# Relation messages in 32 matmuls instead of 48 a tile, with two serial adds on VectorE, and five long loops set at the head of a fetch block

## The chip, the cores and the metric

The kernel runs on one core of one Trainium2 chip. The metric is device microseconds of the whole kernel, one launch. A core has TensorE (PE, with its weight loads shown apart as PEld), VectorE (DVE), ScalarE (ACT), GpSimd (POOL) and the queue engine SP.

## The reference

A graph layer with eight relations, then a mixture of 16 experts with the best two chosen for each node. There are 3125 nodes of 256 features and 53125 edges (50000 drawn ones, both ways of 25000, and one loop for each node), sorted by target.

```
h_all = einsum('ni,roi->rno', layernorm(x), weight)          # 8 relations
messages = segment_sum(h_all[edge_type, src], dst, nodes)
x = x + messages + bias
t = layernorm(x)
probs = softmax(t @ gate_w + gate_b);  best two, weights rescaled to sum 1
h = silu(t @ w1[e]) * (t @ w2[e]);     out = sum over the two of weight * (h @ w3[e])
x = x + out
```

## The kernel before

**Gather stage.** The sum over edges is taken before the product with the relation weights. The nodes are cut into 25 tiles of 125 (`TILES`, `TP`), the sorted edges into 425 chunks of 125, 17 to a turn (`TC`), in six groups of 3, 3, 3, 3, 3 and 2 chunks (`GROUPS`). For each chunk POOL issues one indirect DMA (L486) that gathers 125 rows of the layernormed table `x_tab`, as two float16 halves, into `got`. VectorE builds a one-hot matrix `hot` of target and relation (L877). TensorE multiplies the two into PSUM (`window`, L1253, 12 matmuls for a group of three chunks). VectorE adds the window's sums to the buffer `store` (`add_window`, L895), and right behind that copies the next indices of that group from `gidx` to `idx` (L897), for which POOL waits before it gathers the group of the next turn. So no group is gathered before the add of the group that used its place.

**One turn** i of the loop has the groups (i,3), (i,4), (i,5), (i+1,0), (i+1,1), (i+1,2). When the last add of a tile is done, ScalarE takes the tile's sums out of `store` as the high half (`take_tile`, L634, 128x2048, into `part`), VectorE makes the low half from the rest (`low_tile`, L909, eight instructions), and TensorE multiplies both with the relation weights (`messages`, L1265): 8 relations, 2 halves of the contraction, and three products each, high by weight-high, high by weight-low, low by weight-high, all summed into 256 columns of one PSUM bank. In `add_tile` VectorE then adds that bank to `acc` (L918), takes mean and variance (L921, L924), later normalizes (L928, L932), and TensorE makes the gate logits (L1280, L1286). ScalarE moves the buffer on (L641) and clears its tail (L612).

**Order on the engines.** Everything is written by hand with semaphores, and each engine works in program order. TensorE's turn is: windows (i,3), (i,4), (i,5), transposes, window (i+1,0), gate, messages of tile i-1, windows (i+1,1), (i+1,2). VectorE's turn is: `low_tile` and the adds of (i,3), (i,4), (i,5), (i+1,0), (i+1,1), then `add_tile`, then the add of (i+1,2). ScalarE's take of the next tile waits for that add and for the messages (`tile_summed`). Turns 2 to 23 are a hardware loop of 22 rounds on each of TensorE, VectorE and ScalarE; turn 1 and the last one are written out. POOL's loop has one turn's 17 gathers as its body. The last turn has no groups of a next tile, and takes the messages of two tiles one behind the other.

**Expert stage.** Rows are sorted by expert into `xs_tab`, and for 58 slots of 128 rows TensorE makes the up products (L1387), transposes (L1395, L1355) and the down products (L1369). It is a loop over pairs of slots on TensorE, VectorE and ScalarE.

The lines that decide the order within `turn` on VectorE:

```python
if at == len(groups) - 1 and parts and not last:
    add_tile(n, node_tile(i - 1, b, single))
if at == 0 and parts:
    low_tile(n)
    buffer_moved(v0 + i)
add_window(v0, t, g, w, v0 + i, second if at < HALF else first)
```

Of the kernel before, what the change touches and what calls it, by code (L numbers as in the profile page):

```python
# [30 lines left out]
ALU = mybir.AluOpType  # L31
# [4 lines left out]
NODES, DIM, RELS = 3125, 256, 8  # L36
# [3 lines left out]
KT = DIM // P  # L40
HT = HIDDEN // P
TP = 125
TILES = NODES // TP
# [47 lines left out]
def build(nc, x, src, dst, etype, w_rel, b_rel, gate_w, gate_b, w1, w2, w3, out):  # L91
# [5 lines left out]
    with ExitStack() as ctx:  # L97
# [3 lines left out]
        def sem(name):  # L101
            return ctx.enter_context(nc.semaphore(name))
# [13 lines left out]
        acc = sb("acc", [TP, TILES, DIM])  # L116
# [22 lines left out]
        wT = part_flat[:, 0:4 * RO].rearrange("p (h k n) -> p h k n", h=2, k=KT)  # L139
# [101 lines left out]
        ps = ctx.enter_context(nc.psum_tensor("ps", [P, 8, QW], F32))  # L241
# [48 lines left out]
        tile_high = sem("tile_high")  # L290
        tile_low = sem("tile_low")
        tile_summed = sem("tile_summed")
        acc_added = sem("acc_added")
        stats2_raw = sem("stats2_raw")
        stats2_begun = sem("stats2_begun")
# [169 lines left out]
        def _(pool):  # L465
# [26 lines left out]
            gather_turn(0)  # L492
            pool.wait_ge(counts_ready, 5)
            visits = pool.value_load(n_visits[0:1, 0:1], min_val=TILES, max_val=TILES * TILES * GEN_W)
            with pool.Fori(1, visits) as n:
                gather_turn(n)


# [51 lines left out]
            pairs = pool.value_load(pairs_i[0:1, 0:1], min_val=EXPERTS // 2, max_val=SLOT_TILES // 2)  # L550
# [22 lines left out]
        def _(act):  # L573
# [27 lines left out]
            for n in range(8):  # L601
                k, rp = n // 4, n % 4
# [53 lines left out]
            with act.Fori(0, tiles_n) as b:  # L656
                with act.Fori(0, wins_n) as w:
                    v0 = (b * GEN_W + w) * TILES
                    move_on(v0, (v0 + 1) * NG + HALF)
                    clear_old(v0)  # L660
                    spread(v0)
                    move_on(v0 + 1, (v0 + 2) * NG + HALF)
                    keep_x2(v0, 0, b)
                    clear_old(v0 + 1)
                    with act.Fori(2, TILES - 1) as i:
                        spread(v0 + i - 1)
                        move_on(v0 + i, (v0 + i + 1) * NG + HALF)
                        keep_x2(v0 + i - 1, i - 1, b)
                        clear_old(v0 + i)
                    t = TILES - 1  # L670

                    take_tile(v0 + t, (v0 + t + 1) * NG, last_high)
                    spread(v0 + t - 1)
                    keep_x2(v0 + t - 1, t - 1, b)
                    spread(v0 + t)
                    keep_x2(v0 + t, t, b)
                    shift(v0 + t)
                    clear_old(v0 + t)
# [42 lines left out]
            pairs = act.value_load(pairs_i[0:1, 0:1], min_val=EXPERTS // 2, max_val=SLOT_TILES // 2)  # L721
            high_xs(0, 0)
            expert_tile(0, 0, first=True)
            expert_tile(0, 1)
            with act.Fori(1, pairs) as i:
                for u in range(2):
                    expert_tile(i, u)
            act.wait_ge(y_done, final_j + 1)
# [8 lines left out]
        def _(dve):  # L737
# [13 lines left out]
            v = nc.vector  # L751
# [161 lines left out]
            def tile_at(table, tile):  # L913
                return table[0:TP, bass.ds(tile, 1), :].rearrange("p a d -> p (a d)")

            def add_tile(n, tile, bank=MSG_BANK):
                dve.wait_ge(tile_summed, n + 2)
                v.tensor_tensor(tile_at(acc, tile), tile_at(acc, tile), ps[0:TP, bank, 0:DIM], ALU.add).then_inc(acc_added, 1)  # L918
                dve.wait_ge(acc_added, n + 2)
                dve.sem_inc(stats2_begun, 1)  # L920
                v.bn_stats(stat2[0:TP, :], tile_at(acc, tile)).then_inc(stats2_raw, 1)  # L921
                dve.wait_ge(stats2_raw, n + 1)
                dve.sem_inc(stats2_begun, 1)
                v.bn_aggr(mv2[0:TP, :], stat2[0:TP, :]).then_inc(stats2_done, 1)  # L924
# [94 lines left out]
            with dve.Fori(0, tiles_n) as b:  # L1019
                with dve.Fori(0, wins_n) as w:  # L1020
# [12 lines left out]
                    dve.wait_ge(bias_added, (b * GEN_W + w + 1) * X_LOADS)  # L1033
                    dve.sem_inc(stats2_begun, 1)
                    turn(v0, 1, b, w, norm=False)
                    with dve.Fori(2, TILES - 1) as i:
                        turn(v0, i, b, w)
                    turn(v0, TILES - 1, b, w, last=True)
                    n = v0 + TILES - 1
# [145 lines left out]
                step(v.tensor_tensor(mtx[:, :], wts[:, 1, :], is_low[:, 1 - k, :], ALU.mult))  # L1185
                step(v.tensor_tensor(wts2[:, k, :], wts2[:, k, :], mtx[:, :], ALU.add))
            v.tensor_copy(pos2[0:TP, :, :], low_hi[:, :, :]).then_inc(pos2_done, 1)
            with dve.Fori(1, pairs) as i:
                for u in range(2):
                    expert_tile(i, u)  # L1190
            low_hid(final_j)
# [15 lines left out]
        def _(pe):  # L1207
# [49 lines left out]
            def messages(n, bank=MSG_BANK, high=tileT[:, 0, :, :, :], low=tileT[:, 1, :, :, :]):  # L1257

                pe.wait_ge(tile_low, n + 2)
                if bank == MSG_BANK:  # L1260
                    pe.wait_ge(acc_added, n + 1)
                for r in range(RELS):
                    for k in range(KT):
                        for a, b in PARTS:
                            last = mm(ps[:, bank, 0:DIM], (high, low)[a][:, k, r, :], wT[:, b, k, r * DIM:(r + 1) * DIM],  # L1265
                                      start=(r == 0 and k == 0 and a + b == 0), stop=(r == RELS - 1 and k == KT - 1 and a == 1))
                last.then_inc(tile_summed, 1)

            def ranks(t0, t1):
# [149 lines left out]
            turn_xs(0, 0, first=True)  # L1419
            expert_tile(0, 0, first=True)  # L1420
            expert_tile(0, 1)
            with pe.Fori(1, pairs) as i:
                for u in range(2):
                    expert_tile(i, u)
            turn_hid(final_j)
# [21 lines left out]
```

## Time and profile before

| what | value |
|---|---|
| time, median of 3 runs | 1306.32 us (1306.45, 1306.32, 1300.31) |
| time of the profiled execution | 1302.33 us |
| its span, first to last instruction | 1300.6 us |
| mean granted TensorE clock | 0.789 of full |
| busy PE / DVE / ACT / POOL | 65% / 47% / 27% / 52% |

The span is one execution, the table's time is that execution's own. Clock is in parts of 2.4 GHz. Busy shares are means over stages with different limits; no engine is busy all the time, so it is the waits that have to be read.

### The profile page before, as it was taken

Reading aid. Unit: us, or ns where it says so; the run is one execution under the profiler, and the core shown is the slowest. Engines: PE = TensorE matmul, PEld = TensorE weight load, DVE = VectorE, ACT = ScalarE, POOL = GpSimd, SP = SyncE. Lnnn points to the kernel's source line nnn. Section 1 sums busy time; section 2 is a strip of 40 time slices with the busy share of each in tenths; the row PEclk is TensorE's granted clock in tenths of the full one; section 3 lists DMA queues with packets and bytes.
Section 4 is the critical chain, followed back from the end, with each engine's and each line's share of the span. In section 5 each row is a group of like instructions: output and inputs, shape, how many; then the busy total and the mean of one; then the engine's idle time right before and its main releaser. Section 6 shows DMA issues by size and latency. Waiting matters only on the chain.

```text
span 1300.6 us, 19171 instructions
## 1 busy us (share of the span) xinstructions
PE 845.9 (65%) x4904; PEld 689.7 (53%) x4905; DVE 607.5 (47%) x1597; ACT 345.9 (27%) x397; POOL 670.0 (52%) x621
## 2 busy tenths in 40 slices
PE   1256677766677766677666677437897988897600
PEld 1134455555555545555555556326786877786500
DVE  6655454445555444444545555674333333333432
ACT  4502223333222222222333323312222222222100
POOL 1366455554555555545555452056444477738373
PEclk9967777777777777777877777658998988999855
DMA  9523333333333222232222321316625364454244
GB/s 223 168 88 107 102 97 102 103 105 108 118 96 96 77 77 76 76 90 69 77 77 77 88 69 33 117 51 224 202 73 185 97 196 158 150 194 109 82 132 124
DMA packets 93629, 145.98 MB, mean 112 GB/s; under 512 B 13367, under 2 KB 67595, under 8 KB 93610
## 3 DMA queue, kind: packets, MB, share of 16 engines
q0 software_dynamic: 25968, 70.94, 18.9%
q1 hardware_dynamic: 50794, 59.48, 14.3%
q10 hardware_dynamic: 16848, 15.34, 3.6%
q8 instruction: 7, 0.11, 0.0%
q14 instruction: 12, 0.10, 0.0%
HBM read 109.90 MB, written 33.98 MB: 111 GB/s over the span
## 4 chain that ended last, share of the span: by engine, by line
PE 22%; issue 19%; DVE 18%; another core or an unknown queue 16%; ACT 8%; DVEq 7%; DMA 5%; POOL 4%; ACTq 1%; SPq 0%; POOLq 0%
PE ps L1387 6%; PE ps L1265 5%; ACT part L634 5%; PE ps L1369 4%; DVE part L909 4%; PE ps L1253 4%; DVE hot L877 3%; DMA y_tab<-ffn 3%; DVE store L895 3%; DVEq L895 2%; POOL x_sb L556 2%; POOL store L567 1%; PE ps L1395 1%; ACT hot L592 1%
## 5 line engine op out<-in xcount | busy, mean ns | idle before, releaser
L486 POOL DMA_INDIRECT got<-x_tab,idx x425 | 405.2, 953 | 379.2 <-DVE idx L897 237.8
L1253 PE MATMUL ps<-hot,got 125*128 125x256 f16 x1700 | 296.5, 328 | 135.8 <-issue 125.1
L1253 PEld LDWEIGHTS ps<-hot,got 125*128 125x128 f16 x1700 | 187.6, 115 | 236.5 <-issue 187.6
L895 DVE TENSOR_TENSOR store<-store,ps 128x512 f32 x150 | 102.8, 685 | 293.2 <-remote 151.0
L1265 PE MATMUL ps<-part 128*128 128x256 f32 x1152 | 191.2, 341 | 24.8 <-DVE part L909 24.8
L1265 PEld LDWEIGHTS ps<-part 128*128 128x128 f32 x1152 | 186.4, 251 | 27.4 <-DVE part L909 27.3
L1387 PE MATMUL ps<-part,operands 128*128 x696 | 183.6, 415 | 1.2 <-DVE operands L1142 1.2
L1387 PEld LDWEIGHTS ps<-part,operands 128*128 128x128 f32 x696 | 134.0, 199 | 28.3 <-issue 1.8
L909 DVE SCALAR_TENSOR_TENSOR part<-store,part 128x256 fp32r<-128x256 f32 x192 | 103.0, 613 | 66.6 <-ACT part L634 42.1
L619 ACT ACTIVATE dev<-mv,eps 125x1 f32<-125x1 f32 x25 | 7.4, 294 | 474.0 <-DVE mv L924 474.0
L1369 PE MATMUL ps<-part,operands 128*128 x696 | 103.4, 301 | 39.1 <-DVE operands L1152 34.5
L877 DVE TENSOR_SCALAR hot<-key_row,pass,drel 125x256 f16<-125x256 f16 x425 | 122.1, 351 | 6.0 <-issue 6.0
L1369 PEld LDWEIGHTS ps<-part,operands 128*128 128x128 f32 x696 | 92.0, 202 | 42.9 <-issue 42.8
L634 ACT ACTIVATE part<-store 128x2048 fp32r x24 | 94.2, 3926 | 63.4 <-DVE store L895 63.4
L509 POOL TENSOR_TENSOR part<-store,part 128x2048 fp32r<-128x2048 f32 (+1 forms) x28 | 97.8, 3493 | 2.3
L507 POOL TENSOR_SCALAR part<-store 128x2048 fp32r<-128x2048 f32 (+1 forms) x28 | 41.5, 1482 | 103.1 <-PE ps L1387 87.1
L699 ACT CAST operands<-ps 128x512 fp32r<-128x512 f32 x58 | 34.1, 587 | 193.7 <-DVE ffn L1148 123.8
L1152 DVE TENSOR_TENSOR operands<-ps,operands 128x512 fp32r<-128x512 f32 x58 | 40.1, 691 | 81.8 <-ACT operands L699 76.9
L1286 PE MATMUL ps<-gw_sb,x2T 128*125 128x16 f32 x100 | 21.9, 336 | 79.5 <-ACT x2T L628 79.5
L520 POOL DMA_INDIRECT x_sb<-x_tab,oct_idx x64 | 61.1, 954 | 23.4 <-issue 17.1
L1148 DVE COPY ffn<-ps 128x256 f32<-128x256 f32 x58 | 24.6, 424 | 90.3 <-PE ps L1369 42.5
L1286 PEld LDWEIGHTS ps<-gw_sb,x2T 128*125 128x125 f32 x100 | 19.3, 273 | 86.8 <-ACT x2T L628 86.8
(198 smaller groups left out, 743.7 us busy)
## 6 DMA issues: line engine op xcount, KB each, us to landing
store<-in_L_ffn_w SPq DMA_DIRECT2D x48, 512.0 KB
xs_tab<-x_sb SPq DMA_DIRECT2D x16, 512.0 KB
y_tab<-ffn SPq DMA_DIRECT2D x9, 896.0 KB
ffn<-xs_tab ACTq DMA_DIRECT2D x59, 128.0 KB
y_tab<-ffn ACTq DMA_DIRECT2D x58, 128.0 KB
got<-x_tab,idx POOLq DMA_INDIRECT x425
acc<-in_x SPq DMA_DIRECT2D x5, 560.0 KB
x_tab<-got SPq DMA_DIRECT2D x5, 560.0 KB
```

The costliest lines, as they stand in the source:

```text
L486: nc.gpsimd.indirect_dma_start(got[:, c, :], None, x_tab, bass.IndirectOffsetOnAxis(ap=idx[:, c:c + 1], axis=0)).then_inc(gathered[c], 16)
L507: nc.gpsimd.tensor_scalar(high, whole, 1.0, 0.0, ALU.mult, ALU.add).then_inc(split_high, 1)
L509: nc.gpsimd.tensor_tensor(part[:, 2 * k + 1, at:at + cols], whole, high.bitcast(F32), ALU.subtract).then_inc(done, 1)
L520: nc.gpsimd.indirect_dma_start(xg[:, u, :], None, x2_tab, bass.IndirectOffsetOnAxis(ap=oct_idx[:, u:u + 1], axis=0)).then_inc(oct_got[u // ...
L634: nc.scalar.activation(high, buffer(v, 0, P * RELS).rearrange("p k (n r) -> p k r n", r=RELS), ACT.Copy, scale=1.0 / SCALE).then_inc(tile_ ...
L877: v.tensor_scalar(hot[0:CE, g % HOT, c - GROUPS[g][0], :], key_row[0:CE, :], pass0[0:CE, 0:1], drel[0:CE, bass.ds(turn * TC + c, 1)], ALU. ...
L895: v.tensor_tensor(window, window, ps[:, WIN_BANK[g], :].rearrange("p (k n) -> p k n", k=KT), ALU.add).then_inc(win_added, 1)
L909: last = v.scalar_tensor_tensor(out=low[:, k, rels, :], in0=whole_sums[:, rels, :], scalar=1.0 / SCALE, in1=high[:, k, rels, :].bitcast(F3 ...
L1253: last = mm(ps[:, WIN_BANK[g], k * KEYS:(k + 1) * KEYS], got[0:CE, c, a * DIM + k * P:a * DIM + (k + 1) * P], hot[0:CE, g % HOT, c - c0, : ...
L1265: last = mm(ps[:, bank, 0:DIM], (high, low)[a][:, k, r, :], wT[:, b, k, r * DIM:(r + 1) * DIM], start=(r == 0 and k == 0 and a + b == 0), ...
L1369: last = mm(ps[:, Y_BANK, 0:DIM], hidT[:, a, k, :], part3[:, bass.ds(at + b, 1), k, :].rearrange("p a n -> p (a n)"), start=(k == 0 and a ...
L1387: last = mm(ps[:, UP_BANK + w, :], xsT[:, a, k, :], part12[:, bass.ds(at + b, 1), w, k, :].rearrange("p a n -> p (a n)"), start=(k == 0 an ...
```

## The change

The change has three parts.

- `messages`: the high half now multiplies weight-high and weight-low in one matmul of 512 columns into the whole bank (`both`), and the low half adds its product to the bank's second 256 columns. That is 16 matmuls of 512 columns and 16 of 256, for 48 of 256, with 32 weight loads for 48. The columns that pass are 12,288 in both. It is done for all 25 tiles.
- `add_tile`: since the sum now lies in two halves of the bank, VectorE adds them to `acc` one after the other, the second add behind a wait for the first (`high_added`) and one more increment of `stats2_begun`. 25 times.
- Loops: the gather loops of POOL, ScalarE and VectorE, and the expert loops of ScalarE, VectorE and TensorE are made with `head_slot` 0, which sets the first instruction of the body at the head of a block of instructions. TensorE's gather loop had it already.

```diff
@@ gather loop, POOL @@
-            with pool.Fori(1, visits) as n:
+            with nc.Fori(1, visits, engines=bass.OrderedEngineSet([pool.engine]), head_slot={pool.engine: 0}) as n:
                 gather_turn(n)
@@ gather loop, VectorE (ScalarE alike, and the three expert loops alike) @@
-                    with dve.Fori(2, TILES - 1) as i:
+                    with nc.Fori(2, TILES - 1, engines=bass.OrderedEngineSet([dve.engine]), head_slot={dve.engine: 0}) as i:
                         turn(v0, i, b, w)
@@ add_tile @@
                 dve.wait_ge(tile_summed, n + 2)
-                v.tensor_tensor(tile_at(acc, tile), tile_at(acc, tile), ps[0:TP, bank, 0:DIM], ALU.add).then_inc(acc_added, 1)
+                v.tensor_tensor(tile_at(acc, tile), tile_at(acc, tile), ps[0:TP, bank, 0:DIM], ALU.add).then_inc(high_added, 1)
+                dve.wait_ge(high_added, n + 1)
+                dve.sem_inc(stats2_begun, 1)
+                v.tensor_tensor(tile_at(acc, tile), tile_at(acc, tile), ps[0:TP, bank, DIM:], ALU.add).then_inc(acc_added, 1)
                 dve.wait_ge(acc_added, n + 2)
@@ messages @@
+                both = ps[:, bank, :].rearrange("p (h d) -> p h d", h=2)
                 for r in range(RELS):
                     for k in range(KT):
-                        for a, b in PARTS:
-                            last = mm(ps[:, bank, 0:DIM], (high, low)[a][:, k, r, :], wT[:, b, k, r * DIM:(r + 1) * DIM],
-                                      start=(r == 0 and k == 0 and a + b == 0), stop=(r == RELS - 1 and k == KT - 1 and a == 1))
+                        mm(both, high[:, k, r, :], wT[:, :, k, r * DIM:(r + 1) * DIM],
+                           start=(r == 0 and k == 0), stop=False)
+                        last = mm(ps[:, bank, DIM:], low[:, k, r, :], wT[:, 0, k, r * DIM:(r + 1) * DIM],
+                                  start=False, stop=(r == RELS - 1 and k == KT - 1))
                 last.then_inc(tile_summed, 1)
```

On TensorE, in the body of the gather loop, the place between window (i+1,0) and window (i+1,1) read before (`part` is the tile's high or low half, `ps` PSUM, and REGISTER_ALU and ISA are the sequencer's own steps):

```order
L1247 ISA
L1249 ISA
L1253 MATMUL ps<-hot,got 128x256 x12
L1265 MATMUL ps<-part 128x256 x48
L1246 REGISTER_ALU
L1247 REGISTER_ALU
L1253 MATMUL ps<-hot,got 128x256 x12
```

and begins now, the pair of the fourth and fifth row coming 16 times:

```order
L1251 ISA
L1253 ISA
L1257 MATMUL ps<-hot,got 128x256 x12
L1269 MATMUL ps<-part 128x512
L1271 MATMUL ps<-part 128x256
L1269 MATMUL ps<-part 128x512
L1271 MATMUL ps<-part 128x256
```

Nothing but the messages themselves moved; the windows stand where they stood.

On VectorE the end of a turn, from the one-hots ahead of `add_tile` to the add of window (i+1,2), read before:

```order
L877 TENSOR_SCALAR hot<-key_row,pass,drel 125x256 x2
L918 ISA
L918 TENSOR_TENSOR acc<-acc,ps 125x256
L921 BN_STATS stat<-acc 125x6
L924 BN_AGGR mv<-stat 125x2
L892 REGISTER_ALU
L893 REGISTER_ALU
L895 REGISTER_ALU x2
L895 ISA
L895 TENSOR_TENSOR store<-store,ps 128x2x256
```

and reads now:

```order
L878 TENSOR_SCALAR hot<-key_row,pass,drel 125x256 x2
L919 ISA
L919 TENSOR_TENSOR acc<-acc,ps 125x256
L922 TENSOR_TENSOR acc<-acc,ps 125x256
L925 BN_STATS stat<-acc 125x6
L928 BN_AGGR mv<-stat 125x2
L893 REGISTER_ALU
L894 REGISTER_ALU
L896 REGISTER_ALU x2
L896 ISA
L896 TENSOR_TENSOR store<-store,ps 128x2x256
```

One row of work came in, between the first add and the statistics, and everything behind it moved down by one.

## Rows read from the trace of the kernel before

**Rows 1.** One turn by windows: us, busy time of PE, PEld, DVE, ACT, POOL, clock, DMA

```profile
470.80:500.90 30.10, 20.09 (x124) 15.61 (x122) 14.49 (x43) 8.66 (x7) 16.11 (x18) 0.77 0.25 74
```

**Rows 2.** Waits over the whole span: total us, times, longest

```profile
DVE store L895 <- remote: 151.0, 13, 12.2
```

**Rows 3.** Timeline of VectorE, one turn: start, us, work, idle before and releaser

```profile
494.31 0.69 DVE L895 TENSOR_TENSOR store<-store,ps 128x512 f32 x1 [11.95 <-remote]
...
495.51 0.41 DVE L918 TENSOR_TENSOR acc<-acc,ps 125x256 f32 x1
496.09 0.43 DVE L921 BATCH_NORM_STATS2 stat<-acc 125x6 f32 x1 [0.16 <-DVE acc L918]
...
497.23 0.69 DVE L895 TENSOR_TENSOR store<-store,ps 128x512 f32 x1 [0.38 <-issue]
497.84 0.21 DVE L897 COPY idx<-gidx 125x3 int32 x1
497.94 0.16 DVE L928 RECIPROCAL rstd<-dev 125x1 f32<-125x1 f32 x1
...
502.30 4.29 DVE L909 SCALAR_TENSOR_TENSOR part<-store,part 128x256 fp32r<-128x256 f32 x8 [2.72 <-issue]
506.50 0.69 DVE L895 TENSOR_TENSOR store<-store,ps 128x512 f32 x1
```

**Rows 4.** Timeline of ScalarE, the same turn

```profile
498.17 3.93 ACT L634 ACTIVATE part<-store 128x2048 fp32r x1 [0.99 <-DVE store L895]
```

**Rows 5.** Timeline of POOL, the first and eleventh gather, and the next first

```profile
477.91 0.95 POOL L486 DMA_INDIRECT got<-x_tab,idx  x1 [4.99 <-DVE idx L897]
...
490.49 0.95 POOL L486 DMA_INDIRECT got<-x_tab,idx  x1 [0.30 <-issue]
...
508.06 0.95 POOL L486 DMA_INDIRECT got<-x_tab,idx  x1 [4.99 <-DVE idx L897]
```

**Rows 6.** Timeline of TensorE, the same turn, messages and one window matmul

```profile
476.50 7.51 PE L1265 MATMUL ps<-part 128*128 128x256 f32 x48 [0.75 <-DVE part L909]
...
488.65 0.28 PE L1253 MATMUL ps<-hot,got 125*128 125x256 f16 x1 [0.43 <-issue]
```

**Rows 7.** Timeline of the last loop turn, gathers and VectorE's wait

```profile
779.30 0.95 POOL L486 DMA_INDIRECT got<-x_tab,idx  x1 [4.99 <-DVE idx L897]
...
788.11 0.95 POOL L486 DMA_INDIRECT got<-x_tab,idx  x1 [0.30 <-issue]
...
791.46 0.69 DVE L895 TENSOR_TENSOR store<-store,ps 128x512 f32 x1 [7.71 <-remote]
```

**Rows 8.** Timeline of another loop turn, TensorE and VectorE

```profile
243.62 3.96 PE L1253 MATMUL ps<-hot,got 125*128 125x256 f16 x33
...
253.27 0.69 DVE L895 TENSOR_TENSOR store<-store,ps 128x512 f32 x1 [12.17 <-remote]
```

**Rows 9.** Timeline of TensorE in the expert stage

```profile
953.30 3.02 PE L1387 MATMUL ps<-part,operands 128*128 x12
956.15 0.38 PE L1355 MATMUL ps<-ident,ffn 128*128 128x128 f32 x2
956.29 1.62 PE L1369 MATMUL ps<-part,operands 128*128 x12
957.74 0.60 PE L1395 MATMUL ps<-ident,ffn 128*128 128x128 f32 x4
```

**Rows 10.** Clock of that stretch, by windows, columns as in the first group

```profile
950.00:975.00 25.00, 25.00 (x156) 22.07 (x155) 10.32 (x19) 7.22 (x15) 15.91 (x11) 1.00 0.24 77
```

**Rows 11.** Page, part 3: instruction queues, packets, MB, share

```profile
q8 instruction: 7, 0.11, 0.0%
q14 instruction: 12, 0.10, 0.0%
```

**Rows 12.** Timeline of the gather stage's end

```profile
815.44 8.53 PE L1265 MATMUL ps<-part,operands 128*128 128x256 f32 x48 [3.63 <-DVE operands L909]
...
825.72 0.42 DVE L918 TENSOR_TENSOR acc<-acc,ps 125x256 f32 x1
```

More of the change, by code:

```diff
@@ L292, in build @@
         tile_summed = sem("tile_summed")
+        high_added = sem("high_added")
         acc_added = sem("acc_added")
@@ L664, in _ @@
                     clear_old(v0 + 1)
-                    with act.Fori(2, TILES - 1) as i:
+                    with nc.Fori(2, TILES - 1, engines=bass.OrderedEngineSet([act.engine]), head_slot={act.engine: 0}) as i:
                         spread(v0 + i - 1)
@@ L724, in _ @@
             expert_tile(0, 1)
-            with act.Fori(1, pairs) as i:
+            with nc.Fori(1, pairs, engines=bass.OrderedEngineSet([act.engine]), head_slot={act.engine: 0}) as i:
                 for u in range(2):
@@ L1187, in _ @@
             v.tensor_copy(pos2[0:TP, :, :], low_hi[:, :, :]).then_inc(pos2_done, 1)
-            with dve.Fori(1, pairs) as i:
+            with nc.Fori(1, pairs, engines=bass.OrderedEngineSet([dve.engine]), head_slot={dve.engine: 0}) as i:
                 for u in range(2):
@@ L1421, in _ @@
             expert_tile(0, 1)
-            with pe.Fori(1, pairs) as i:
+            with nc.Fori(1, pairs, engines=PE_ONLY, head_slot={pe.engine: 0}) as i:
                 for u in range(2):
```

## The prediction

> **What bounds the kernel now.** I read the kernel by stages first and then one loop turn engine by engine. A turn of the gather loop takes 30.10 us, and in it no engine is busy throughout: TensorE 20.1 us, POOL 16.1, VectorE 14.5, ScalarE 8.7 [rows 1]. So the turn is a ring of waits, and the question is which. The list of waits puts one on top that no engine of the page explains: VectorE's window add stands still before a releaser called remote, up to 12.2 us at a time [rows 2], and the timeline shows the same wait once a turn, 11.95 us in the one that I take as specimen [rows 3]. There are 22 such loop turns, the starts of which lie 30.10 to 30.19 us apart.
>
> The ring can be walked. VectorE wakes at 494.31, adds window (i+1,1), adds the messages at 495.51, takes the statistics at 496.09 and 496.67, and adds window (i+1,2) at 497.23 [rows 3]. That add releases ScalarE, which takes the tile from 498.17 for 3.93 us [rows 4]. VectorE's eight instructions of the low half start at 502.30, right behind it, and take 4.29 us, the next window add follows at 506.50 and its index copy at 507.09 [rows 3]. That copy releases POOL, which starts its burst of gathers at 508.06 after 4.99 us of idleness [rows 5]. In the turn before the same burst began at 477.91, and its eleventh gather started at 490.49, so they follow at 12.58/10 = 1.26 us; then POOL stops, and VectorE wakes 3.82 us after that last start [rows 3, 5].
>
> What VectorE waits for is TensorE: the messages and window (i+1,1). But the messages' records end at 476.50 + 7.51 = 484.01 [rows 6], more than 10 us before VectorE wakes. Two other turns show that the wake hangs on the burst of gathers, not on the matmuls. In the last loop turn only 8 gathers are issued, 779.30 to 788.11, and the wait is 7.71 us in place of 11.95 [rows 7], so 4.24 us less for three gathers less, which are 3 x 1.26 = 3.8 us. The wake there is 791.46 - 788.11 = 3.35 us after the last gather's start, near the 3.82. And in another turn TensorE ran through 33 window matmuls by 243.62 + 3.96 = 247.58, and VectorE still woke only at 253.27, after 12.17 us [rows 8]. So TensorE's completion reaches VectorE only when POOL's burst is over. I don't know the mechanism; the rows show the order. The period then is: burst of 11 gathers and its tail, 494.31 - 477.91 = 16.4 us, plus VectorE, ScalarE, VectorE from wake to the next burst, 508.06 - 494.31 = 13.75 us. They add up to 30.15.
>
> **The change part by part.**
>
> *The second add.* It lies between 495.51 and 496.09, inside the 13.75 us. Each instruction behind it waits for its result, and the window add that releases ScalarE stands behind all of them on VectorE. Its price is one step of this chain. The nearest row is the add itself with the wait behind it: 496.09 - 495.51 = 0.58 us, of which 0.41 is the add [rows 3]. The statistics behind it, also a dependent step, take the same 0.58 (496.09 to 496.67). The lower bound is 0.41, if the wait for the first add costs nothing; the upper one 0.58 + 0.16 = 0.74, if the additional increment costs another of the gaps seen there. I take 0.58. Can it hide? The idle time of 0.38 us ahead of 497.23 is sequencer work (four register steps stand there in the listing) that begins only when the last wait has passed, so it moves along. ScalarE has nothing else that ends later, VectorE's own idle time of 2.72 us ahead of 502.30 is a wait for ScalarE and starts and ends later too. POOL's second burst, from 495.86, hangs on a copy ahead of the add and isn't touched; it has 4.99 us of slack before the next burst, which becomes 5.57. So the whole 0.58 goes into each period. 22 loop turns and the written-out turn 1 give 23 x 0.58 = 13.3 us. At the end of the stage two more tiles are added; for the last one the add at 825.72 stands behind its messages [rows 12] and ahead of the last layernorm, so one more 0.58, while the other add lies beside the messages from 815.44 on and costs nothing. Sum: **+13.9 us**, bounds 24 x 0.41 = 9.8 and 24 x 0.74 = 17.8.
>
> The Trainium skill ("VectorE: DVE Perf Modes", the section on the TRN2 errata) speaks against this part: each VectorE instruction pays a fixed extra latency, so one tile cut in two pays it twice. By its cycle table an add of 256 columns from PSUM is (120 + 256)/0.96 = 392 ns, by my estimate from that page 24 x 0.39 = 9.4 us in sum; the row has 410 ns for the instruction and 0.58 us for the step with its wait, and the sum above goes by the row.
>
> *The joined messages.* In the expert stage at granted clock 1.00 (2.4 GHz) [rows 10], twelve 512-column matmuls pass in 956.15 - 953.30 = 2.85 us, 0.2375 each, and twelve of 256 columns in 957.74 - 956.29 = 1.45 us, 0.121 each [rows 9]. So a tile's messages go from 48 x 0.121 = 5.81 us to 16 x 0.2375 + 16 x 0.121 = 5.74 us: 0.07 us. In the loop turns they run at mixed clock, 7.51 us, and end 10 us before the wait that follows them ends. The gain is hidden there. At the end of the stage the messages of the last tile are on the path, 8.53 us for 48 at the lower clock [rows 12], 0.178 each; columns are the same, so the bounds are 0 and, if every removed instruction were worth a fixed part of it, 16 x (0.178 - 256/1200 x 0.5) = 1.1 us per tile. I take 0.2 for both last tiles: **-0.2 us**.
>
> *The loop heads.* If a loop lay badly across blocks of instructions, this would show at its back edge or on the instruction queues. VectorE passes its back edge between 497.84 and 497.94, two instructions 0.10 us apart, closer than the 0.21 us of the first [rows 3]. POOL's gathers stand at one pitch throughout. The queues of instructions moved 7 and 12 packets in the whole span [rows 11], far fewer than the 22 rounds. So there is nothing to gain in a round. Each loop is entered once, past some padding; if an entry costs a fetch, that is six times at most 1 us from a full wait of the kind of 0.3 to 1 us seen at entries. The lower bound is a gain of nothing, the upper 6 us; most entries lie beside other engines' waits. I take **+1**.
>
> Sum: 13.9 - 0.2 + 1 = 14.7 us. On the profiled execution's own 1302.33 us (span 1300.6) that gives 1317.0; that execution lies 4.0 us under the median of the runs, from which one gets 1321.0. Two of the three runs lie at 1306.4 and one at 1300.3, so I set the forecast between the two, at **1319 us**.
>
> **The rivals.**
>
> *The shorter messages let TensorE's signals through (faster).* 32 fewer instructions (16 matmuls, 16 weight loads) stand per tile between window (i+1,0) and window (i+1,1). If what holds the completion back is a full queue ahead of TensorE that drains slowly under the burst, fewer entries could let window (i+1,1) complete before the burst is over. For it: under the burst TensorE's window matmuls do appear singly, and the wait starts right with the burst. The Trainium skill ("TensorE: Matmul & The Clock Gate", the text on engine queue depths) gives TensorE a queue of 64 entries; a tile's messages were 96 entries and are now 64. Against it: in the turn of rows 8 the matmuls were through at 247.58 and the wake still came at the burst's end. Its price: VectorE would wake up to when the windows are ready, bounded by POOL, whose 17 gathers at 1.26 us take 21.4 us; a turn could fall from 30.1 to some 22 to 24, 6 us x 22 = -132 us, so about 1185 with the added step. If only the two or three last entries matter, 2 us a turn, 1319 - 44 = 1275. It decides from 0.58 us a turn on. Chance 0.14.
>
> *The second add finds cover (no change).* If the wake in fact follows something that doesn't hang on VectorE's chain, say ScalarE's or the clock of the DMA queues, the 0.58 goes into VectorE's 11.95 us of idleness. Then +0 to +3 from the entries: 1303 to 1309. For it: that idleness is large. Against: the burst begins with the index copy (4.99 us of idleness before it, released by it), and the wait shrank when the burst was shorter. Chance 0.12.
>
> *The loop heads do more than nothing.* If the loops' position matters each round, by fetch stalls hidden in the gaps called issue, 0.3 us a round for 22 + 28 rounds is 15 us, in either sign, since a head moved is also a tail moved. The Trainium skill ("Runtime: NRT & Kernel Launch", the section on instruction fetch) has a taken branch out of the two blocks at hand stall for a fetch. The 19 instruction packets of the span are too few for that in 50 rounds. As a gain it would cancel the add: 1304, chance 0.04; as a loss, 1334, chance 0.04.
>
> **How the numbers follow.** The forecast case has the rest, 0.66, and its own range from 1302.33 + 9.8 - 2.2 = 1310 to 1306.32 + 17.8 + 5 = 1329. The range for 8 in 10 leaves out the case of the passed signals (0.14) and the loss by loop heads (0.04), and reaches down to the no-change case: 1303 to 1329. Half a percent, 6.5 us, is about what a measurement of this kernel can tell from no change: slower than 1312.9 counts as slower. Slower: 0.66 less a sliver of 0.03 that stays under the bound, and the 0.04, 0.67. Same: 0.12 + 0.04 + 0.03, less a part that falls faster, 0.18. Faster: 0.15.
>
> **What would show it.** The two adds should stand 0.58 us apart once a turn, and the idle time of VectorE before a remote releaser should stay at 11.9 us, the eleven gathers at 1.26 us, the turn at 30.7 us. The messages' record of a turn should be as long as now within 0.3 us. A remote wait shorter than 11 us with the burst unchanged would prove the first rival; turns of 30.1 us the second; instruction packets in the hundreds or gaps at the loops' ends the third. I would be wrong most widely if fewer entries in TensorE's queue unblock the windows.

## The result, and the profile after

The changed kernel takes 1314.83 us (median of 5 runs, 1310.95 to 1316.49), the kernel before 1305.49 us in its 5 runs beside it. The ratio is 1.0074 with a 95% interval of 1.0053 to 1.0095: slower, by 9.3 us. The profiled execution took 1315.28 us with a span of 1313.6 us, 13.0 us over the span before. The forecast was 1319 us, in a range of 1303 to 1329.

The experiments need one thing more: the machine was found in two conditions. The kernel before took 1300 to 1306 us in the runs of this section, and 1296 to 1311 us beside e7 to e10; beside e1 to e6 it took 1056 to 1067 us. The runs of one kernel that were timed together lie within 1.4% of each other. Every comparison below is within one condition, and they are called **the 1300 condition** and **the 1060 condition**.

One turn of the loop after, by windows (us, busy PE, PEld, DVE, ACT, POOL, clock, DMA share, GB/s):

```profile
478.00:508.55 30.55, 20.64 (x105) 15.00 (x103) 14.95 (x44) 8.72 (x7) 16.19 (x18) 0.75 0.25 73
```

VectorE in that part of the timeline, which answers to [rows 3]:

```profile
501.64 0.69 DVE L896 TENSOR_TENSOR store<-store,ps 128x512 f32 x1 [11.80 <-PE ps L1257]
...
502.85 0.41 DVE L919 TENSOR_TENSOR acc<-acc,ps 125x256 f32 x1
503.41 0.42 DVE L922 TENSOR_TENSOR acc<-acc,ps 125x256 f32 x1
503.98 0.43 DVE L925 BATCH_NORM_STATS2 stat<-acc 125x6 f32 x1
...
505.12 0.69 DVE L896 TENSOR_TENSOR store<-store,ps 128x512 f32 x1 [0.38 <-issue]
...
510.17 4.28 DVE L910 SCALAR_TENSOR_TENSOR part<-store,part 128x256 fp32r<-128x256 f32 x8 [2.65 <-issue]
```

And POOL, which answers to [rows 5], with the first gather of the last loop turn [rows 7]:

```profile
485.39 0.95 POOL L487 DMA_INDIRECT got<-x_tab,idx  x1 [5.51 <-DVE idx L898]
...
497.98 0.94 POOL L487 DMA_INDIRECT got<-x_tab,idx  x1 [0.30 <-issue]
...
515.91 0.95 POOL L487 DMA_INDIRECT got<-x_tab,idx  x1 [5.50 <-DVE idx L898]
...
791.00 0.95 POOL L487 DMA_INDIRECT got<-x_tab,idx  x1 [5.51 <-DVE idx L898]
```

The profile names TensorE's window as the releaser here, and "remote" in the turn of [rows 3]; in the kernel before it puts the same wait of 11.9 us down to either in about half of the turns, so the name says nothing.

The two adds start 0.56 us apart, the statistics 0.57 us behind the second. From wake to next burst it is 515.91 - 501.64 = 14.27 us where it was 13.75; the medians over the loop's turns are 14.28 and 13.75. But from the burst's first gather to the wake it is 501.64 - 485.39 = 16.25 us where it was 16.40: the burst is as long as before (12.59 us from first to eleventh), and the time from the eleventh gather to the wake is 3.66 us for 3.82. In the medians it is 16.27 for 16.39 us, and 3.70 for 3.82. Over ten turns the period is (791.00 - 485.39)/10 = 30.56 us, before (779.30 - 477.91)/10 = 30.14: 0.42 us a turn, 9.2 us in 22.

The rest of the 13.0 us lies around the loop. The first gather starts 0.48 us later (48.77 for 48.29). From it to the last loop turn it takes 11.2 us more, 2.0 more than the 9.2; 0.9 us of that lie in the first three turns, and most of the rest in two neighbouring turns of the after-trace, which together took 1.3 us more than two others. The end of the stage, from 791.00 to the last add at 837.34, is not longer (46.3 us for 46.4). The expert stage up to the last down products is 1.2 us longer (1237.41 for 1224.62).

The messages, which answer to [rows 6], are now pairs; the first and the last of a turn's 32:

```profile
483.99 0.79 PE L1269 MATMUL ps<-part 128*128 128x512 f32 x1 [1.16 <-DVE part L910]
...
492.07 0.28 PE L1271 MATMUL ps<-part 128*128 128x256 f32 x1
```

8.36 us, for 7.51, both at mixed clock. That is the scatter of single turns: over 20 turns of each trace the median is 8.08 us for 8.05, with 7.1 to 8.7 us in single ones. There is no gain, and the records end more than 9 us ahead of the wake in either.

### The profile page after: what moved, and what is told of

Its sections match the earlier page's. It is cut to its first block, busy times and chain, and to the rows that moved or that the text cites. A ratio compares the mean times of both kernels' runs of the same rounds, so it can differ in the third digit from the quotient of the medians.

```text
span 1313.6 us, 18427 instructions
## 1 busy us (share of the span) xinstructions
PE 841.9 (64%) x4504; PEld 660.7 (50%) x4505; DVE 619.2 (47%) x1622; ACT 344.9 (26%) x397; POOL 670.6 (51%) x621
## 4 chain that ended last, share of the span: by engine, by line
PE 25%; DVE 19%; issue 18%; another core or an unknown queue 16%; DVEq 7%; DMA 6%; POOL 3%; ACT 3%; ACTq 1%; SPq 0%; POOLq 0%
PE ps L1393 7%; PE ps L1257 5%; PE ps L1375 5%; DMA y_tab<-ffn 4%; PE ps L1269 4%; DVE part L910 4%; DVE hot L878 4%; DVEq L896 2%; PE ps L1271 2%; POOL x_sb L557 2%; DVE store L896 2%; POOL store L568 2%; PE ps L1401 1%; ACT part L635 1%
## 5 line engine op out<-in xcount | busy, mean ns | idle before, releaser
L1257 PE MATMUL ps<-hot,got 125*128 125x256 f16 x1700 | 288.4, 328 | 135.3 <-issue 106.2
L1269 PE MATMUL ps<-part 128*128 128x512 f32 x384 | 186.5, 509 | 25.1 <-DVE part L910 25.1
L1271 PE MATMUL ps<-part 128*128 128x256 f32 x384 | 129.1, 336 | 0.0
L1269 PEld LDWEIGHTS ps<-part 128*128 128x128 f32 x384 | 97.2, 253 | 52.3 <-DVE part L910 27.6
L1271 PEld LDWEIGHTS ps<-part 128*128 128x128 f32 x384 | 97.4, 254 | 0.0
```

Source lines behind the costliest of these rows:

```text
L1257: last = mm(ps[:, WIN_BANK[g], k * KEYS:(k + 1) * KEYS], got[0:CE, c, a * DIM + k * P:a * DIM + (k + 1) * P], hot[0:CE, g % HOT, c - c0, : ...
L1269: mm(both, high[:, k, r, :], wT[:, :, k, r * DIM:(r + 1) * DIM], start=(r == 0 and k == 0), stop=False)
L1271: last = mm(ps[:, bank, DIM:], low[:, k, r, :], wT[:, 0, k, r * DIM:(r + 1) * DIM], start=False, stop=(r == RELS - 1 and k == KT - 1))
```

## The experiments

### The 1060 condition: each part alone

`e1_heads` is the kernel before with the loop heads. They are six, and not five as the title has it: those of the gather loops of POOL, ScalarE and VectorE, and those of the expert loops of ScalarE, VectorE and TensorE. `e2_no_heads` is the changed kernel without them.

> The kernel before with the six loop heads alone. My theory (the heads do nothing in a round): turn of the gather loop stays at 30.14 us, the time within 2 us of the kernel before (ratio 0.999 to 1.002). Rival (the heads cost or give something each round): with the chain of the second add taken off, a turn would move by 0.1 us or more, 2.5 us or more in the gather stage, or the expert stage would by 1 us.

> The changed kernel without the loop heads: joined messages and the two adds. My theory: all of the loss is here, turn 30.55 us, +9 to +12 us over the kernel before, ratio 1.007 to 1.009. Rival (heads carry part of it): +6 us or less.

`e3_extra_add` leaves the 48 messages as they were and gives `add_tile` a second, dependent add of zeros:

```diff
-                v.tensor_tensor(tile_at(acc, tile), tile_at(acc, tile), ps[0:TP, bank, 0:DIM], ALU.add).then_inc(acc_added, 1)
+                v.tensor_tensor(tile_at(acc, tile), tile_at(acc, tile), ps[0:TP, bank, 0:DIM], ALU.add).then_inc(high_added, 1)
+                dve.wait_ge(high_added, n + 1)
+                dve.sem_inc(stats2_begun, 1)
+                v.tensor_tensor(tile_at(acc, tile), tile_at(acc, tile), zero[0:TP, 0:1].to_broadcast([TP, DIM]), ALU.add).then_inc(acc_added, 1)
```

> The kernel before, its 48 messages unjoined, with a second dependent add on VectorE (of zeros) behind the first. My theory (the step on the ring costs 0.57 us a turn, and the shorter messages take 0.12 to 0.15 back): wake to next burst 14.3 us, tail of the burst 3.82 us, turn 30.70 us, +12.5 to +14 us. Rival (the tail shrank by chance or for another reason than the messages): turn 30.55 us, like the changed kernel.

`e4_one_add` is the changed kernel, heads included, with the second add left out.

> The changed kernel with only the first of the two adds; it leaves out the sum of the bank's second half (high by weight-low and low by weight-high). My theory: wake to next burst back at 13.75 us, tail 3.70 us, turn 30.0 us, so 2 to 4 us faster than the kernel before (ratio 0.997 to 0.999). Rival (the loss comes from the 512-column matmuls or the heads, not from the add): turn above 30.3 us.

Both kernels were also run unchanged, again in the 1060 condition:

> The kernel before, unchanged, for its trace beside the other runs of this chip. The four runs so far were all some 240 us faster than the trace before: POOL issues its 425 gathers there without a pause and no remote wait stands in a turn. Theory: the state goes with the chip, and this trace shows the same as they do, turns of about 22.1 us, a span of 1056 to 1066 us. If it shows turns of 30.1 us, the state is not the chip's.

> The changed kernel, unchanged. If POOL issues without a pause as in the four runs, the turn is bounded by the larger of POOL's 17 gathers (22.07 us in the run with one add) and the ring with the second add (22.65 us in the runs with two): 22.6 us a turn, and a ratio of 1.011 to 1.013 like the run without heads; if the heads cost the 6 us that their run alone seemed to show, 1.016 to 1.018. With turns of 30.5 us: 1.007.

| kernel | heads | adds | messages | ratio to before (95%) | turn, us |
|---|---|---|---|---|---|
| b_again | no | 1 | 48 | (one run, 1055.56 us) | 22.00 |
| e1_heads | yes | 1 | 48 | 1.0063 (1.0037 to 1.0088) | 22.09 |
| e4_one_add | yes | 1 | 32 | 1.0055 (1.0028 to 1.0083) | 22.07 |
| e2_no_heads | no | 2 | 32 | 1.0115 (1.0084 to 1.0145) | 22.61 |
| e3_extra_add | no | 2 | 48 | 1.0116 (1.0084 to 1.0148) | 22.65 |
| a_again | yes | 2 | 32 | 1.0197 (1.0160 to 1.0233) | 22.54 |

A turn is here the start of gather 409 less that of gather 35, over 22. Each ratio is against the kernel before that was timed beside it; for a_again that was another set of runs than for e1 to e4. A second add costs 0.5 to 0.65 us a turn and 1.15%, with joined messages or without. The joined messages alone give nothing (e2 against e3, e4 against e1). The heads cost 0.6%, some 6 us, and a turn with them is as long as one without, within 0.1 us. Together that is 1.8%, and a_again's 2.0% agrees within its interval.

The turns of 30 us that I had expected did not occur here. Of the times, e1 (expected within 2 us) and e4 (expected 2 to 4 us faster) both came out 6 us slower, e2 came out 12.7 us slower where I expected 9 to 12, and e3, at 12.7 us, lay in its 12.5 to 14. What e3 was to tell of the tail of the burst it could not, since this condition has no such tail.

What bounds a turn here? One turn of the kernel before by windows, and VectorE's window add that had the remote wait:

```profile
311.40:333.40 22.00, 15.67 (x123) 13.28 (x122) 14.96 (x44) 9.86 (x7) 16.82 (x18) 0.90 0.45 130
```

```profile
438.93 0.69 DVE L895 TENSOR_TENSOR store<-store,ps 128x512 f32 x1 [3.10 <-PE ps L1253]
```

The wait is 3.10 us for 11.95, POOL pauses nowhere in the loop for more than 0.3 us, where it paused 4.99 in [rows 5], and no wait called remote is in the list of waits. With the second add POOL does stand still once in the turn shown. POOL and VectorE of `e3_extra_add`:

```profile
443.30 0.94 POOL L487 DMA_INDIRECT got<-x_tab,idx  x1 [1.22 <-DVE idx L898]
```

```profile
430.23 0.41 DVE L919 TENSOR_TENSOR acc<-acc,ps 125x256 f32 x1
430.79 0.43 DVE L922 TENSOR_TENSOR acc<-acc,zero 125x256 f32 x1 [0.15 <-DVE acc L919]
431.36 0.43 DVE L925 BATCH_NORM_STATS2 stat<-acc 125x6 f32 x1
```

So with one add the turn sits at POOL's issue (17 gathers at 1.25 us, two or three of them longer, 22.0 us), and with two the ring of VectorE and ScalarE is just longer (22.6 us). That is a reading of the traces; the run that was to test it, e9, fell in the other condition. The step is 0.56 us in this condition too.

### Where the heads cost

The 6 us do not lie in the gather loop. From the last add to the last down products e1, e4, e6 and a_again take 372 to 376 us, and b_again, e2, e3 and e5, which have no heads, take 362 to 370. Slot by slot it is one step: from VectorE's copy of the first slot's result to its copy of the second's it takes 11.6 to 12.8 us with heads and 6.4 to 7.2 us without; the median slot takes 4.8 to 4.9 us in all of them. ScalarE and VectorE there, of `a_again`:

```profile
711.40 0.59 ACT L700 CAST operands<-ps 128x512 fp32r<-128x512 f32 x1 [8.02 <-issue]
```

```profile
712.31 0.69 DVE L1156 TENSOR_TENSOR operands<-ps,operands 128x512 fp32r<-128x512 f32 x1 [4.79 <-ACT operands L700]
```

and ScalarE of `e2_no_heads`:

```profile
705.47 0.59 ACT L700 CAST operands<-ps 128x512 fp32r<-128x512 f32 x1 [3.05 <-DVE ffn L1152]
...
711.89 0.59 ACT L700 CAST operands<-ps 128x512 fp32r<-128x512 f32 x1 [3.69 <-DVE ffn L1152]
```

In the one ScalarE stands still for 8 us as its loop begins; in the other it has done a slot meanwhile. The records of the loops' own lines show what happens. The branches of `a_again` in the two loops, from the view of one source line (count, shortest, median and longest ns, first and last start in us):

```profile
L726 ACTq COMPARE_BRANCH  x29: 40/45/55, 705.3 to 1011.4; - x29
```

```profile
L1192 DVEq COMPARE_BRANCH  x29: 47/56/69, 707.4 to 1010.5; - x29
```

and those of `e2_no_heads` in ScalarE's:

```profile
L726 ACTq COMPARE_BRANCH  x28: 40/45/50, 716.5 to 1003.2; - x28
```

With a head there is one branch more, and it is at the entry. Behind it ScalarE's sequencer records nothing for 5.92 us (705.33 to 711.25) and VectorE's nothing for 4.73 us (707.47 to 712.20), and the next record of either is a register operation that waits for no semaphore. In the five traces with ScalarE's head this gap is 5.5 to 5.9 us, in the six with VectorE's (e7 is one) 4.5 to 5.7 us. Behind the entries of the other four loops with a head it is at most 0.7 us. So two entries stall, one beside the other, and VectorE's ends 0.9 to 1.9 us after ScalarE's.

The changed kernel shows the same in the 1300 condition, and the kernel before shows something else at that place. ScalarE after:

```profile
903.87 0.59 ACT L700 CAST operands<-ps 128x512 fp32r<-128x512 f32 x1 [9.01 <-issue]
```

ScalarE before:

```profile
888.51 0.59 ACT L699 CAST operands<-ps 128x512 fp32r<-128x512 f32 x1 [3.31 <-remote]
895.62 0.60 ACT L708 ACTIVATE ffn<-ps 128x512 f32<-128x512 f32 x1 [6.53 <-remote]
```

To see whether ScalarE's head is the cause I took that one alone back:

> The changed kernel with all loop heads but the one of ScalarE's expert loop. All four traces with heads have ScalarE standing still for 8 to 9 us ahead of L700 in the second slot, called issue, and the step from the first to the second slot takes 12 us or more where it takes 6.4 to 7.2 us without heads. Theory: ScalarE's entry into its expert loop, past the padding, costs it some 6 us once. Then this kernel shows a step of 6.4 to 7.2 us, and 5 to 7 us less than the changed kernel on the same chip (ratio to before 1.012 to 1.014 with POOL without a pause). Rival (another engine's head, or each round pays a little): step stays at 12 us, ratio 1.018 to 1.021.

This run fell in the 1300 condition. Ratio 1.0068 (1.0043 to 1.0093) against 1.0074 of the full change: nothing gained. ScalarE of `e7_no_act_head`:

```profile
898.40 0.59 ACT L700 CAST operands<-ps 128x512 fp32r<-128x512 f32 x1 [4.47 <-remote]
...
905.54 0.60 ACT L709 ACTIVATE ffn<-ps 128x512 f32<-128x512 f32 x1 [6.55 <-remote]
```

and VectorE:

```profile
903.95 0.69 DVE L1156 TENSOR_TENSOR operands<-ps,operands 128x512 fp32r<-128x512 f32 x1 [5.03 <-issue]
```

The 9.01 us of issue are gone from ScalarE, so its head does make its stall. But VectorE kept its head and its stall. And ScalarE has the kernel before's wait of 6.5 us again, which falls on eight gathers that POOL issues at that time, and which ends 1.6 us after VectorE's stall. In the 1300 condition the stalls of both heads lie beside that wait and cost nothing that shows. So e7 could not tell the price of ScalarE's head. What is shown is that the six heads together cost 6 us in the 1060 condition (e1). That it is these two entries follows from the place and the size, and as the two stalls overlap, taking one back would not give 6 us either; no run in the 1060 condition took one back alone.

The Trainium skill ("Runtime: NRT & Kernel Launch", the section on instruction fetch) says that a taken branch to a target outside the two blocks at hand has to wait for a fetch. The traces agree with it. In all five traces with ScalarE's head a packet of 8 KB on the instruction queue q14 starts 1.5 to 1.8 us ahead of ScalarE's first record behind the gap, and in the six with VectorE's one starts 1.9 to 2.0 us ahead of VectorE's; e7 has only the second, and `e2_no_heads` has no such packet from 701 to 710 us. The page of the changed kernel counts four more on that queue, and one fewer on q8, than [rows 11]:

```profile
q14 instruction: 16, 0.13, 0.0%
```

### The second add off the ring

`e8_adds_behind` is the changed kernel without heads, in another order. `e9_before_adds_behind` is the kernel before in that order.

```diff
 VectorE, turn:
-                    if at == len(groups) - 1 and parts and not last:
-                        add_tile(n, node_tile(i - 1, b, single))
                     ...
                     add_window(v0, t, g, w, v0 + i, second if at < HALF else first)
+                    if at == len(groups) - 1 and parts and not last:
+                        add_tile(n, node_tile(i - 1, b, single))
 ScalarE, loop:
-                        spread(v0 + i - 1)
-                        move_on(v0 + i, (v0 + i + 1) * NG + HALF)
+                        move_on(v0 + i, (v0 + i + 1) * NG + HALF, v0 + i - 1)   # take, then spread, then shift
```

VectorE also builds its one-hots ahead of `normalize2` now.

> Joined messages and two adds, no heads, but the adds and statistics behind the add of window (i+1,2), ScalarE's square root behind its take, VectorE's one-hots ahead of the normalization. This takes four steps of 0.57 us off the ring and puts some 1.1 us of normalization into it. Theory (the second add costs because it stands on the ring): in turns of 22.6 us the ring falls under POOL's 22.07 us and the turn goes to 22.07 to 22.15, ratio to before 1.000 to 1.003, where the same kernel with the adds ahead had 1.0115. In turns of 30 us: 1.2 us less a turn than with the adds ahead. Rival (the cost is the add's work, not its place): 22.65 us, ratio 1.011.

> The kernel before with the same order: one add, behind the window add. Theory: where POOL issues without a pause the turn stays at POOL's 22.05 us, so no change within 0.3%. In turns of 30.1 us: 0.6 us less a turn, 14 us (ratio 0.988 to 0.992). Rival (POOL is not the bound in these turns but the ring is at 22.05 by chance): 21.4 to 21.5 us a turn, 12 us less.

Both ran beside e7 in the 1300 condition, and both are faster than the kernel before: 0.9834 (0.9799 to 0.9870) and 0.9866 (0.9835 to 0.9896). A turn is 1.3 us shorter where I expected 1.2, and 0.8 where I expected 0.6. VectorE of `e8_adds_behind`:

```profile
486.44 0.69 DVE L896 TENSOR_TENSOR store<-store,ps 128x512 f32 x1 [11.86 <-remote]
...
487.83 0.69 DVE L896 TENSOR_TENSOR store<-store,ps 128x512 f32 x1
...
488.50 0.42 DVE L919 TENSOR_TENSOR acc<-acc,ps 125x256 f32 x1
489.07 0.42 DVE L922 TENSOR_TENSOR acc<-acc,ps 125x256 f32 x1 [0.15 <-DVE acc L919]
...
493.66 4.30 DVE L910 SCALAR_TENSOR_TENSOR part<-store,part 128x256 fp32r<-128x256 f32 x8
```

and ScalarE:

```profile
488.76 3.90 ACT L635 ACTIVATE part<-store 128x2048 fp32r x1 [20.73 <-DVE store L896]
```

The window add stands 1.39 us behind the wake, where it stood 3.48 (505.12 - 501.64); ScalarE's take runs while VectorE adds. Of the 2.1 us that this takes off, 0.8 come back, which I put down to the normalization that now stands in the ring. From wake to the next burst it is 499.42 - 486.44 = 12.98 us, 1.3 less than after. The turn is 29.25 us (median of the loop's turns) against 30.55 in e7. With the order changed, the kernel with two adds and 32 messages (29.25 us) is no slower than the one with one add and 48 (29.38). From wake to the next burst both take the same, 12.99 us and 13.00 us in the medians, where after and before had 14.28 and 13.75. So the second add costs only where it stands on the ring. The 0.13 us between the turns are the tail of the burst: 3.69 to 3.71 us from the last gather to the wake in the three kernels with 32 messages in this condition, 3.81 and 3.82 in the two with 48. These three also have the second add, so that it is the messages that shorten the tail is likely, but no run separates the two.

### The burst

If VectorE's wake hangs on the end of POOL's burst, fewer gathers in the burst must bring it earlier. In `e5_late_copy` (kernel before), `e6_late_copy_changed` and `e10_behind_late_copy` (on e8) group 0's indices are copied together with group 1's:

```diff
-                v.tensor_copy(idx[0:CE, c0:c1], gidx[...c0, c1 - c0)]).then_inc(idx_ready, 1)
+                if g > 0:
+                    first_c = 0 if g == 1 else c0
+                    v.tensor_copy(idx[0:CE, first_c:c1], gidx[...first_c, c1 - first_c)]).then_inc(idx_ready, 2 if g == 1 else 1)
```

> The kernel before with the index copy of group (i+1,0) joined to that of (i+1,1), so that POOL's burst before VectorE's wake has 8 gathers for 11, and 9 behind it. In turns of 30.1 us: my theory (the wake hangs on the end of the burst) gives 3.8 us less a turn, 26.3 us, some 80 us less in all (ratio 0.93 to 0.95); the rival (TensorE's matmuls bound the wake) gives no change. In turns of 22 us, where POOL is without a pause: the copy comes before POOL has done the 8, so no change within 3 us, or up to 1 us a turn slower if it comes late.

> The changed kernel with the same joined copy. In turns of 30.5 us: 26.7 us a turn, the difference to the other kernel with the joined copy still 0.4 us a turn. In turns of 22.6 us: as the changed kernel within 3 us, or up to 1 us a turn slower.

These two fell in the 1060 condition, which has no burst with a pause behind it, and say nothing on it: 1.0028 (1.0013 to 1.0044) and 1.0270 (1.0251 to 1.0290, where a_again had 1.0197). The joined copy cost 4 us on the kernel before and 8 us on the changed one.

> The kernel with the adds behind the window add, and the index copy of group (i+1,0) joined to that of (i+1,1): POOL issues 8 gathers ahead of VectorE's wake and 9 behind it. In turns with the remote wait (29.25 us before this edit): theory (the wake hangs on the end of POOL's burst) 3 x 1.26 = 3.8 us less, 25.4 to 25.8 us a turn, the remote wait 8.0 to 8.2 us, some 80 us less in all (ratio 0.92 to 0.93); rival (the wake hangs on TensorE's matmuls) 29.2 us, ratio 0.983. In turns without the remote wait: POOL-bound, 22.1 to 22.5 us, ratio 1.000 to 1.010.

This one fell in the 1300 condition: 0.9851 (0.9824 to 0.9878) where e8 had 0.9834. No 80 us. POOL of `e10_behind_late_copy`:

```profile
473.95 0.95 POOL L487 DMA_INDIRECT got<-x_tab,idx  x1 [0.31 <-issue]
479.05 0.95 POOL L487 DMA_INDIRECT got<-x_tab,idx  x1 [4.15 <-DVE idx L900]
...
488.55 1.26 POOL L487 DMA_INDIRECT got<-x_tab,idx  x1 [0.30 <-issue]
490.12 0.95 POOL L487 DMA_INDIRECT got<-x_tab,idx  x1 [0.30 <-DVE idx L900]
```

and VectorE:

```profile
477.48 0.69 DVE L896 TENSOR_TENSOR store<-store,ps 128x512 f32 x1 [2.54 <-PE ps L1259]
...
498.37 0.34 DVE L878 TENSOR_SCALAR hot<-key_row,pass,drel 125x256 f16<-125x256 f16 x1 [1.14 <-issue]
499.07 0.35 DVE L878 TENSOR_SCALAR hot<-key_row,pass,drel 125x256 f16<-125x256 f16 x1 [0.36 <-issue]
500.47 0.34 DVE L878 TENSOR_SCALAR hot<-key_row,pass,drel 125x256 f16<-125x256 f16 x1 [1.05 <-issue]
```

The burst did not get shorter: the nine gathers behind the wake last until the next index copy, so that they and the next eight follow without a pause, and a turn has one burst of 17. My expectation failed there in a way that I should have read from the rows: nine gathers take 11.3 us, and from the wake to the next copy there were 12.0, less 1.6 until POOL starts.

But the long wait is gone: VectorE's idle time before this add has a median of 3.1 us, where it had 11.8 in e8. And the wake no longer stands at one distance from the burst's last gather. What it follows instead can be read from TensorE's records. In the turn of [rows 3] the last matmul of window (i+1,1) is this one of the kernel before:

```profile
487.24 0.27 PE L1253 MATMUL ps<-hot,got 125*128 125x256 f16 x1 [0.44 <-issue]
```

It ends at 487.51, and VectorE, which waits for it, wakes at 494.31. The trace's own records of the two semaphores say the same: the messages' one moves at 493.69 and the window's at 493.82, 9.7 and 6.3 us behind the ends of the matmuls that move them. The ends of matmuls are modelled, but not by microseconds, as the other traces show. Over the 22 loop turns of each trace:

| traces | end of the window's last matmul to VectorE's wake, us | start of the last gather to the wake, us |
|---|---|---|
| before, after, e7, e8, e9 (1300 condition) | medians 7.4 to 9.0, none under 2.6 | medians 3.7 to 3.8, single turns from 0.1 to 3.9 |
| b_again, a_again, e1 to e6 (1060 condition) | 0.50 in every turn | 0.0 to 1.2 |
| e10 (1300 condition) | 0.50 to 0.52 in 20 turns of 22, 1.4 and 8.4 in the others | 2.2 to 9.2, median 6.3 |

So in the 1300 condition with a pause behind the burst, TensorE's completions do reach VectorE late, when the burst is over. The 0.1 is one turn in each of the three kernels with 32 messages: there the wake comes 5 us early, inside the burst, and the turn behind it takes 37 us for 30, so the first rival happened once in 22 turns and won nothing. In e10 they reach it at once, as in the 1060 condition, and the wake waits for the matmuls themselves. What was won went elsewhere: a tile's messages take 12.7 us in the median where they took 7.5 in e8, and in the second half of the long burst VectorE itself goes in steps of 0.70 us or twice that, with nothing to wait for. The turns take 26 to 32 us, 29.0 in the mean.

## Why the prediction was right, and where it was off

The forecast time was 4 us too high and the forecast change, 14.7 us, was 5.4 us too large: 9.3 us were measured, with an interval of 6.9 to 12.4. The mechanism of the largest term was right, its sum was not.

*What bounds the kernel.* The ring was the right picture for the runs that were predicted: its part from wake to burst grew by the step that was added to it, and the order of e8 took out what it should. That TensorE's completions reach VectorE only at the end of the burst is borne out by the five traces of this form in the 1300 condition, where the wake stands 3.7 to 3.8 us behind the last gather. It is no rule of that condition: in e10, with a burst of 17, the wake follows TensorE's own records.

*The second add.* Right in mechanism. Forecast 0.58 us a turn, and measured 0.56 between starts, 0.53 in the ring. It hid nowhere; e3 has the whole cost with none of the rest of the change, and e8 takes it away by its place alone. The sum for it was 13.9 us, of which 22 x 0.58 = 12.8 for the loop turns; these brought 9.2.

*The joined messages.* The term "-0.2 us, hidden in the loop turns" is the one that was mis-sized. In the 1300 condition the tail of the burst is 0.12 us a turn shorter with the 32 fewer instructions on TensorE, 2.6 us in 22, which is most of what the forecast was too high in the turns. If it is the messages, and not the second add, that shorten the tail, this is the first rival at a fiftieth of its price: it had 6 us a turn and came to 0.12. The Trainium skill ("TensorE: Matmul & The Clock Gate", on queue depths) has 64 entries in TensorE's queue, and 64 is what a tile's messages now take; the trace shows no release at that number. In the 1060 condition the joining is worth nothing that shows.

*The last tiles.* One step of 0.58 us was charged to the end of the stage, and the trace shows none (46.3 us for 46.4).

*The loop heads.* "+1, bounds 0 and 6" fits the runs predicted, where the expert stage is 1.2 us longer and the stalls that the heads bring lie beside the remote wait. That is luck: in the 1060 condition the same heads cost 6 us, the upper bound. The bound was made from six entries of 1 us each, and no row of the kernel before shows such an entry; there are two that take 4.5 to 5.9 us, and they overlap. "Nothing in a round" held in all traces, within 0.1 us.

*The second rival*, a cover for the add, was wrong in both conditions. Where POOL's issue seemed to be the bound, the turns still grew by 0.5 to 0.65 us for a step of 0.56, so there was a slack of less than 0.1 us, and not the 0.58 that would have hidden it.

## What to carry to other kernels

Two instructions for one can be right for the engine that is spared and wrong for the one that has to add the halves: count the dependent steps on the ring, at start-to-start distance (0.56 us here for 0.41 us of work), and then look for a place off the ring before giving the change up. Here the same two adds cost 0.5 us a turn ahead of the window add and nothing behind it, and e8 is 1.7% faster than the kernel before in the 1300 condition, most of it from the other steps that moved with the adds: e9, with one add, is 1.3% faster. Whether the new order also helps in the 1060 condition was not run. A loop head moved to a block's start has to be paid at the entry, up to 5.9 us here, and could be worth it only if the rounds were stalling. And a part that lies beside a longer wait cannot be priced by taking it back there: e7 changed ScalarE's stall and not the time.

## What the runs showed of the hardware

The same kernel takes 1060 or 1300 us, steady in runs that are timed together. All of the difference in the gather loop is the late completion: turns of 22.0 us without it and 30.1 with. Between the traces of the kernel before in the two conditions lie 247 us, 201 of them between the first gather and the last add and 46 behind that, and what makes the 46 was not followed up. It isn't the chip's number, since one numbered chip was seen in either condition. What sets it stays open, and so does the mechanism by which POOL's gathers hold back other engines in the one condition. Two forms of it were seen: completions of TensorE that arrive 2 to 10 us late, and slow steps. In e10 VectorE's own instructions went at 0.70 us, which is the step at which TensorE's single matmuls stood in the trace before (486.5 to 493.6 us). A change that is judged in one condition can look different in the other: 0.7% here and 2.0% there.
